# Seven block products in place of eight for the outputs of four tile pairs, with sums of blocks on VectorE

## The reference

```python
def _L0_cond_ref(x, c, weight, c_weight, bias):
    out = lax.conv_general_dilated(x, weight, window_strides=(STRIDE,), padding=[(PAD, PAD)], ..., feature_group_count=GROUPS)
    ctx = jnp.einsum('nd,od->no', c, c_weight)
    return out + ctx[:, :, None] + bias[None, :, None]

def _L0_ffn_ref(x, A_w, B_w, Wq_w, keys):
    q = jnp.einsum('bsd,rd->bsr', x, Wq_w)
    scores = jnp.einsum('bsr,er->bse', q, keys)
    top_vals, top_idx = jax.lax.top_k(scores, TOP_K)
    top_w = jax.nn.softmax(top_vals, axis=-1)
    gate = jnp.sum(jax.nn.one_hot(top_idx, NUM_EXPERTS) * top_w[..., None], axis=-2)
    z = jnp.einsum('bsd,nd->bsn', x, A_w)          # 64 experts of rank 8: 512 columns
    z_gated = (z.reshape(..., 64, 8) * gate[..., None]).reshape(..., 512)
    return jnp.einsum('bsn,on->bso', z_gated, B_w) * SCALING

x = x + _L0_ffn_ref(_L0_cond_ref(x, ...), A_w, B_w, Wq_w, keys)   # x: 32 x 64 x 1024
```

## Time and profile before

| | us |
|---|---|
| median of 3 runs (lowest, highest) | 234.68 (233.78, 234.82) |
| the profiled execution's own time | 234.61 |
| its span, first to last instruction | 232.8 |
| PE busy | 228.6 |
| PE weight loads busy | 204.4 |
| DVE busy | 172.9 |
| ACT busy | 113.2 |

### The profile page before, as it was taken

One profiled execution on the slowest core, in us unless ns is written; L12 is line 12 of the kernel. 1 busy time (PEld: TensorE's weight loads), 2 busy tenths in 40 slices (PEclk: granted clock), 3 DMA queues, 4 the chain that ended last, 5 costly groups with the idle time before them and its releaser, 6 DMA issues.

```text
span 232.8 us, 4002 instructions
## 1 busy us (share of the span) xinstructions
PE 228.6 (98%) x1381; PEld 204.4 (88%) x1381; DVE 172.9 (74%) x411; ACT 113.2 (49%) x293; POOL 7.7 (3%) x16
## 2 busy tenths in 40 slices
PE   8999999999999999999999999999999999999995
PEld 8999998888989989898898989889898989898884
DVE  2699889999878696977969587786958748827232
ACT  4996768265282562728356272735627262221000
POOL 2010071000000000000000000000000000000000
DMA  6999055742825538164553815545381433552632
GB/s 186 373 400 398 34 136 184 290 115 102 235 117 145 175 98 260 58 177 181 137 182 91 270 50 167 192 134 187 89 271 52 117 109 90 184 175 98 182 134 92
DMA packets 23780, 38.79 MB, mean 167 GB/s; under 512 B 2768, under 2 KB 11856, under 8 KB 23760
## 3 DMA queue, kind: packets, MB, share of 16 engines
q1 hardware_dynamic: 23616, 38.45, 50.8%
q10 hardware_dynamic: 144, 0.08, 0.2%
HBM read 25.94 MB, written 12.58 MB: 165 GB/s over the span
## 4 chain that ended last, share of the span: by engine, by line
PE 77%; DVE 15%; issue 3%; DMA 2%; ACT 2%; SPq 1%; DVEq 0%; ACTq 0%
PE p_z L686 30%; PE p_out L724 12%; PE p_out L725 12%; PE p_out L732 12%; PE p_conv L637 10%; DVE h_lo L801 3%; DVE h_t L841 2%; DMA x_blk<-in_x_blocks 2%; DVE a_lo L801 2%; DVE x_lo L801 2%; DVE z_g L926 1%; DVE a_raw L936 1%; ACT h_c L426 1%; ACT x_hi L390 1%; DVE b_lo L801 1%
## 5 line engine op out<-in xcount | busy, mean ns | idle before, releaser
L724 PE MATMUL p_out<-b_hi,zt_hi 128*128 128x512 f32 (+1 forms) x128 | 50.8, 398 | 0.3 <-DVE x_nat L944 0.3
L725 PE MATMUL p_out<-b_hi,zt_lo 128*128 128x512 f32 (+1 forms) x128 | 50.0, 392 | 0.0
L732 PE MATMUL p_out<-b_lo,zt_hi 128*128 128x512 f32 (+1 forms) x128 | 34.3, 391 | 0.0
L686 PE MATMUL p_z<-a_hi,h_hi 128*128 128x264 f32 x240 | 34.1, 285 | 0.1
L686 PE MATMUL p_z<-a_hi,h_lo 128*128 128x264 f32 x240 | 34.2, 285 | 0.0
L686 PE MATMUL p_z<-a_lo,h_hi 128*128 128x264 f32 x240 | 34.0, 284 | 0.0
L686 PEld LDWEIGHTS p_z<-a_hi,h_hi 128*128 128x128 f32 x240 | 31.9, 188 | 1.9 <-issue 0.8
L686 PEld LDWEIGHTS p_z<-a_hi,h_lo 128*128 128x128 f32 x240 | 31.2, 188 | 0.0
L686 PEld LDWEIGHTS p_z<-a_lo,h_hi 128*128 128x128 f32 x240 | 31.1, 188 | 0.0
L724 PEld LDWEIGHTS p_out<-b_hi,zt_hi 128*128 128x128 f32 x128 | 24.1, 188 | 6.0 <-issue 0.4
L732 PEld LDWEIGHTS p_out<-b_lo,zt_hi 128*128 128x128 f32 x128 | 23.8, 188 | 5.7
(11 more groups left out here) (109 smaller groups left out, 280.1 us busy)
## 6 DMA issues: line engine op xcount, KB each, us to landing
x_nat<-in_x_rows SPq DMA_DIRECT2D x16, 512.0 KB, 5.2
out_dram<-x_nat SPq DMA_DIRECT2D x31, 256.0 KB, 3.0
x_blk<-in_x_blocks SPq DMA_DIRECT2D x14, 516.0 KB, 3.6
z_dram<-a_raw SPq DMA_DIRECT2D x64, 64.0 KB, 1.8
...
```

Source lines behind the costliest of these rows:

```text
L686: mm = nc.tensor.matmul(z_bank(t, b)[:, 0:HB], h[:, t % 2, r, :], a[:, r, b * HB:(b + 1) * HB], start=k == 0 and r == 0, stop=k == 2 and r ...
L724: nc.tensor.matmul(dst, zt_hi[:, t % 2, c, :], b_hi[:, c, cols], start=c == 0, stop=False)
L725: nc.tensor.matmul(dst, zt_lo[:, t % 2, c, :], b_hi[:, c, cols], start=False, stop=False)
L732: mm = nc.tensor.matmul(dst, zt_hi[:, t % 2, c, :], b_lo[:, c, start:stop], start=False, stop=c == JC - 1)
```

## The change

Tiles 6 to 13 form four pairs (m = 0 to 3). A pair's gated z, 256 rows by 512, and B, 512 by 1024, are each cut into two by two blocks. In place of eight block products of 6 matmuls each there are seven (`product_1` to `product_7`), by sums of blocks:

- DVE sums blocks of B once (`sum_b`, in iterations 4 to 7), ACT and DVE split the four sums (`split_bt`). SP loads B again for it (`load_b`).
- For each pair DVE sums blocks of z (`sum_z31`, `sum_z2`, `sum_z4`); seven z blocks are split (`split_z1`, `split_z12`, `split_z34`, `split_z22`) where eight were.
- Partial sums that several outputs share are copied from one PSUM bank to another by ACT (`copy_xy`, `copy_yz`, `copy_zx`), and products are added on top of them. `add_5` adds one product to both tiles of the pair; `add_11`, `add_12`, `add_22` and `add_21` follow.
- In the loop, PE does products 1, 5, 2, 6 of pair m in iteration 9+2m and 7, 3, 4 in iteration 10+2m. Iterations 7 and 8 have one half of tile 5 each. `conv_sum` stands between the two banks of z from iteration 4 on.
- Room is made: `x_blk` has two slots from tile 5 on instead of three, `ones` and `cw` lie in `h_t`, `z_g` in `a_raw`, and later weights of the convolution in `h_c`.

The core of the diff:

```diff
+FP = 6
+NP = (NT - 2 - FP) // 2
+TB = 4
+LD = FP + 2 * NP
...
-        x_blk = sb("x_blk", [P, XB, XS + 2 * XO])
+        x_blk = sb("x_blk", [P, XB * XS])
...
+        zt_hi = sb("zt_hi", [P, 7, 2, P], F32R)
+        zt_lo = sb("zt_lo", [P, 7, 2, P], F32R)
+        bt_hi = sb("bt_hi", [P, 4, 2, J], F32R)
+        bt_lo = sb("bt_lo", [P, 4, 2, J], F32R)
...
+        b_sums = (a_raw[:, 3:5, 0:J], a_raw[:, 5:7, 0:J], h_c[:, 0].rearrange("p (a n) k -> p a (n k)", a=2))
+        z_sums = h_c[:, 0].rearrange("p (s tb) x -> p s tb x", s=2)
...
+        def pair_banks(m):
+            if m == NP - 1:
+                return p_conv[:, 0, :], p_conv[:, 1, :], p_conv[:, 2, :], p_t[:]
+            return p_out[:, 0, :], p_out[:, 1, :], p_conv[:, 2, :], p_t[:]
...
+                elif t >= FP + 2:
+                    m = (t - FP - 2) // 2
+                    sp.wait_ge(s_zsum, 3 * m + 3)
+                    sp.wait_ge(*((s_z22lo, m + 1) if t % 2 else (s_z1lo, m + 1)))
...
+            def split_z12(m):
+                if m:
+                    act.wait_ge(s_p6, m)
+                act.wait_ge(s_zsum, 3 * m + 2)
+                high(zt_at(zt_hi, 2, 2), sums_at(1), s_z12hi)
...
+            def split_bt(k):
+                act.wait_ge(s_btsum, k + 1)
+                high(bt_hi[:, k], b_sums[(0, 0, 1, 0)[k]], s_bthi)
+
+            def copy_xy(m):
+                x, y, _, _ = pair_banks(m)
+                act.wait_ge(s_p1, m + 1)
+                if m == 0:
+                    act.wait_ge(s_added, out_count(FP - 1, 1))
+                elif m < NP - 1:
+                    act.wait_ge(s_c12, m)
+                high(y, x, s_xy)
...
                 exp(i)
-                split_z(i - 1)
+                if i >= FP + 4 and i % 2 == 0:
+                    copy_zx(m)
+                if FP + 3 <= i < NT - 1 and i % 2:
+                    copy_xy(m)
+                if i == NT - 2:
+                    copy_xy(NP - 1)
+                if i <= FP:
+                    split_z(i - 1)
+                if i == FP + 1:
+                    split_z1(0)
+                if i >= FP + 2 and i % 2 == 0:
+                    split_z12((i - FP - 2) // 2)
+                if FP + 3 <= i < NT - 1 and i % 2:
+                    split_z34(m)
+                    split_z22(m)
                 if i + 3 < NT:
                     split_x(i + 3)
                 if i in (5, 7):
                     split_w(i // 2)
                     sum_w(i // 2)
-                if i == NT - 3:
-                    take_q(NT - 2)
                 if i + 2 < NT:
                     split_h(i + 2)
+                if TB <= i < TB + 4:
+                    split_bt(i - TB)
+                if FP + 3 <= i < NT - 1 and i % 2:
+                    split_z1(m + 1)
+                    copy_yz(m)
+                if i == NT - 2:
+                    split_z34(NP - 1)
+                    split_z22(NP - 1)
+            copy_yz(NP - 1)
+            split_z(NT - 2)
+            copy_zx(NP - 1)
             split_z(NT - 1)
...
-                            pe.wait_ge(s_zg, 2 * t)
+                            pe.wait_ge(s_zg, 2 * t - 1)
+                    if k == 0 and 1 not in banks and t >= 3:
+                        pe.wait_ge(s_zg, 2 * t)
...
+            def product_5(m):
+                pe.wait_ge(s_z12hi, m + 1)
+                pe.wait_ge(s_z12lo, m + 1)
+                if m:
+                    pe.wait_ge(s_vadd, m)
+                product(pair_banks(m)[2], 2, b_sum(0, m), False).then_inc(s_p5, 1)
...
+                m = (i - FP - 3) // 2
                 for k in range(3):
                     z_product(i, k, (1,), range(R))
+                if TS <= i < NT - 2:
+                    conv_sum(i + 2)
                 z_product(i, 0, (0,), range(R))
                 z_product(i, 1, (0,), range(R))
                 if i < TS:
                     turn_q(i)
                 z_product(i, 2, (0,), range(R))
-                if i + 2 < NT:
+                if i < TS:
                     conv_sum(i + 2)
                 scores(i)
-                if i >= NT - 2:
-                    out_part(i - 3, 1)
-                if i < NT - 1:
+                if i <= FP:
                     out_part(i - 2, 0)
-                if i + 2 < NT:
                     conv_pair(i + 2)
-                if i < NT - 3:
                     out_part(i - 2, 1)
-            out_part(NT - 3, 0)
-            out_part(NT - 3, 1)
-            out_part(NT - 2, 0)
+                elif i <= FP + 2:
+                    out_part(FP - 1, i - FP - 1)
+                    conv_pair(i + 2)
...
+                elif i % 2:
+                    product_1(m)
+                    product_5(m)
+                    conv_pair(i + 2)
+                    product_2(m)
+                    product_6(m)
+                else:
+                    product_7(m)
+                    product_3(m)
+                    conv_pair(i + 2)
+                    product_4(m)
             out_part(NT - 2, 1)
             out_part(NT - 1, 0)
             out_part(NT - 1, 1)
...
+            def sum_z31(m):
+                a = FP + 2 * m
+                dve.wait_ge(s_zi, 16 * (a + 2))
+                step = JQ + 64
+                ends = a_raw[:].rearrange("j r x -> j (r x)")[:, 0:2 * step].rearrange("j (s x) -> j s x", s=2)
+                ends = ends[:, :, 0:J].rearrange("j s (tb x) -> j s tb x", tb=4)[:, :, :, 0:64]
+                nc.vector.tensor_tensor(z_sums[:, :, :, 0:64], ends, zt_half(a + 1, 0).unsqueeze(1).to_broadcast([P, 2, 4, 64]),
+                                        ALU.subtract).then_inc(s_zsum, 1)
+
+            def sum_z2(m):
+                dve.wait_ge(s_zsum, 3 * m + 1)
+                nc.vector.scalar_tensor_tensor(out=z_sums[:, 1, :, 64:P], in0=zt_half(FP + 2 * m, 0), scalar=-1.0,
+                                               in1=z_sums[:, 1, :, 0:64], op0=ALU.mult, op1=ALU.subtract).then_inc(s_zsum, 1)
+
+            def sum_b(k):
+                dst, other = ((0, 1), (0, 2), (1, 2), (0, 1))[k]
+                for load in ((0, 1), (2,), (), (3,))[k]:
+                    dve.wait_ge(s_bt[load], 16)
+                nc.vector.tensor_tensor(b_sums[dst], b_sums[dst], b_sums[other], ALU.add).then_inc(s_btsum, 1)
...
+            def add_5(m):
+                a, cols = FP + 2 * m, slice(J, 2 * J)
+                dve.wait_ge(s_p5, m + 1)
+                dve.wait_ge(*rows_come(a))
+                dve.wait_ge(*rows_come(a + 1))
+                both = x_nat[:, a % XN:a % XN + 2, cols]
+                nc.vector.scalar_tensor_tensor(out=both, in0=pair_banks(m)[2].unsqueeze(1).to_broadcast([P, 2, J]), scalar=-SCALING,
+                                               in1=both, op0=ALU.mult, op1=ALU.add).then_inc(s_vadd, 1)
...
             split_z(1)
+            add(0, 0)
             split_h(4)
-            add(0, 0)
             for i in range(3, NT):
+                m = (i - FP - 3) // 2
                 if i + 3 < NT:
                     differ(i + 3, 0)
                 copy_scores(i)
...
                 if i + 3 < NT:
                     differ(i + 3, 1)
                 take_first(i)
-                if i < NT - 3:
+                if i <= FP + 1:
                     add(i - 3, 1)
+                if FP + 5 <= i < NT - 1 and i % 2:
+                    add_21(m - 1)
                 top_second(i)
                 take_second(i)
                 weigh(i)
                 invert(i)
                 gate(i)
                 turn_z(i)
-                if i >= NT - 3:
-                    add(i - 3, 1)
                 if i + 2 < NT:
                     turn_h(i + 2, 0)
                     turn_h(i + 2, 1)
-                split_z(i - 1)
+                if i <= FP:
+                    split_z(i - 1)
                 if i == 3:
                     split_keys()
                 if i in (5, 7):
                     split_w(i // 2)
                     split_ws(i // 2)
-                add(i - 2, 0)
+                if i <= FP + 1:
+                    add(i - 2, 0)
+                if i == FP + 1:
+                    split_z1(0)
+                if TB <= i < TB + 4:
+                    sum_b(i - TB)
+                if i == FP + 2:
+                    sum_z31(0)
+                    add(FP - 1, 1)
+                    sum_z2(0)
+                    sum_z4(0)
+                elif i >= FP + 4 and i % 2 == 0:
+                    sum_z31(m + 1)
+                    add_12(m)
+                    sum_z2(m + 1)
+                    add_22(m)
+                    sum_z4(m + 1)
+                elif FP + 3 <= i < NT - 1:
+                    add_5(m)
+                    split_z34(m)
+                    split_z22(m)
+                    add_11(m)
+                if i >= FP + 2 and i % 2 == 0:
+                    split_z12((i - FP - 2) // 2)
                 if i + 3 < NT:
                     split_x(i + 3)
                 if i in (4, 6):
                     sum_w(i // 2)
```

(16 more changed lines are left out.)

342 lines of the change are left out of this document (283 added, 59 removed).

## The result

| | before | after |
|---|---|---|
| median, us | 234.59 | 244.44 |
| lowest, highest | 233.78, 234.82 | 242.07, 245.94 |
| profiled execution, span | 234.61, 232.8 | 243.17, 241.3 |
| PE, DVE, ACT busy | 228.6, 172.9, 113.2 | 227.5, 195.5, 126.9 |

The runs of before are those of the prediction and one more beside after. The change makes the kernel slower: ratio 1.0349, 95% interval 1.029 to 1.0407. That ratio is made of the two runs of after with the highest clock (242.07 and 243.17 us). The four runs are ordered by TensorE's mean granted clock: 0.993 gave 242.07 us, 0.986 gave 243.17, and 0.972 gave 245.72 and 245.94. The first two lie inside the stated range of 235.9 to 243.5 us, the other two above it.

The account below looks back on a forecast made before the run. PE bounds the kernel before; after, DVE's cycle to x_lo exceeds PE's shorter iterations. 234.61 - 5.58 (matmuls) - 0.3 (`add(0, 0)`) + 11.75 (waits) = 240.5 us, range 235.9 to 243.5.

Parts of the forecast that it names:

- Direction and mechanism: Slower: DVE's longer list delays x_lo, so PE waits at the third `conv_sum` matmul; chance 0.82 of over 0.5% slower.
- 24 matmuls off PE, 5.58 us: On PE, 42 output matmuls a pair for 48; four pairs at 0.2325 us a matmul save 5.58 us.
- DVE's cycles: From one third `conv_sum` matmul to the next through DVE: 13.46 to 14.46 us in iterations 5 to 12; waits total 11.75.
- a small sum: On DVE, a 256-element sum of z blocks: priced 0.34 us, possibly up to 0.45, as a gating half.
- side remark on records taken as spacing: On DVE, taking the longer record lengths as spacing between starts would add an estimated 1 to 1.5 us.
- x_hi behind zt_hi: On ACT in iterations 8, 10, 12, x_hi stands behind zt_hi; DVE itself would reach x_lo 0.6 us earlier.
- the milder rival: On ACT, x_hi is not held up behind zt_hi: waits 9.5 us, time 238.2; chance 0.20 for 236 to 238.5.
- -0.3 us for `add(0, 0)`: Putting `add(0, 0)` ahead of `split_h(4)` removes the 0.34 us for which PE waited; counted as -0.3 us.
- a sign against it: The prediction is wrong if, among other signs, stretches before 95 us differ from before by over a microsecond.
- The stalls cost more than they last: Rival: PE's waits of 3.2 and 3.6 us lower TensorE's clock, 2.9 us per fall, 246 us; chance 0.04.
- the gain arrives: Rival: DVE's reserve (26 us against 21.6) suffices, x_lo is in time at `conv_sum`, 228.7 us; chance 0.12.
- Edits at nothing: PSUM copies on ACT, the query chain (ends A+2.6, scores at A+3.15) and the tail after the last scores cost nothing.

Follow-up runs that it names:

- experiment 1: Changed kernel plus matmuls nobody reads, ahead of `conv_sum` in iterations 8, 9 (ten each), 11 and 13 (six each); 240.41 us.
- experiment 12: Against 9: bt_hi behind the next iteration's exp on ACT, bt_lo ahead of the next sum_b on DVE, fourth B load moved; 228.72 us.
- experiment 4: Kernel before the change, with only `conv_sum` moved between the banks of z from iteration 4 on; 234.09 us, ratio 0.9984.
- experiment 2: Changed kernel with x_hi ahead of zt_hi on ACT in iterations 8, 10 and 12, nothing else moved; 239.43 us.
- experiment 11: As 9, but with B's sums in iterations 4 to 7, where the change has them; 234.79 us.
- 7: Changed kernel, DVE's list reordered: x_lo first, query steps earlier in even iterations, ACT's `split_z12` behind `split_h`; B's sums in iterations 4 to 7; 234.74 us.
- Experiments 3: Changed kernel with `conv_sum` back behind both banks of z; 238.07 us.
- experiments 5: Changed kernel with x_lo right behind `turn_h` on DVE, and x_hi ahead of the z sums' split on ACT; 239.19 us.
- 8: As 7, but with B's sums one iteration earlier, in iterations 3 to 6; 233.18 us.
- 9: As 8, with `split_q` before `split_h` in every iteration and an add between `turn_q` and `split_q`; 233.35 us.

## Why the prediction was right, and where it fell short

*Direction and mechanism: right.* The forecast was slower, by DVE's longer list ahead of x_lo, with PE standing at the third matmul of `conv_sum`. The time of 240.5 us is 3.9 us under the median of 244.44, which lies 0.9 us above the range; the two runs with the higher clock, 242.07 and 243.17, lie in it. That experiment 1, without a fall of the clock, comes to within 0.1 us of the sum is in part luck: its waits are 0.6 us longer than forecast and its start is some 0.3 us shorter.

- **24 matmuls off PE, 5.58 us.** Experiment 12 bears it out. From the scores of iteration 4 to those of iteration 15 its trace takes 139.41 us, for 144.58 before: 5.17 less. Iterations 8 and 9 pay back 0.7, and moving `conv_sum` gives some 0.4 by itself (experiment 4): 5.58 + 0.4 - 0.7 is 5.3. (The medians, 234.71 and 228.72, are 5.99 us apart; the profiled execution, at 229.51, was the slowest of five.) The spacing of 0.2325 us was the right price.
- **DVE's cycles.** The predicted 14.03, 14.03, 14.46, 14.46, 13.83 and 14.46 us were 14.09, 14.10, 14.56, 14.60, 13.87 and 14.63 with the clock kept up. Six cycles of some twenty pieces each are within 0.17 us. Start-to-start prices from rows add up. The waits that follow from them and the prediction's iterations of PE are 12.33 us for 11.75. One price was low: sum_z2 takes 0.45 us and not 0.34 (126.85 to 127.30 above), the upper value that the prediction gave for a small sum. Its side remark on records taken as spacing was low too: by its own lists they would add some 2 to 3 us and not 1 to 1.5. Nothing rests on it.
- **x_hi behind zt_hi.** Said to cost 0.6 us of DVE's time, and by the prediction's list 1.16 in iteration 8, where there is one add fewer. Experiment 2 took 0.7 to 0.8 off each of the three cycles, 2.2 us together, for 2.3 forecast by the milder rival. In iteration 8 less came off than was listed, since DVE's zt_lo still waits for ACT's zt_hi there and the small sums are dearer. That x_hi would itself release PE, at the first matmul of `conv_sum`, was not foreseen; it does not change the sum.
- **-0.3 us for `add(0, 0)`.** Too small: the scores of iteration 4 come at 64.43 us in after and at 65.55 before. That is 1.1 us, just over the microsecond that the prediction named as a sign against it. The other kernels with the same start have 64.0 to 65.0, so this part also varies by itself. The change has other matmuls on `ones` at the start as well, and no experiment tells the two apart.
- **The clock: the missing term.** The sum counted a wait at its length. "The stalls cost more than they last" was a rival with 0.04. It should have been a term, for the sum itself forecast waits of 3.2 and 3.6 us in two iterations running, a pattern that no row of before contains. Not having seen a fall was taken as evidence against one, where it was only that PE hardly idles in the loop of the kernel before. Its price of 2.9 us a fall was too high for after, where one costs 1.52 us (experiment 1 against after), as the lower level lasts 3.4 us and not for a whole bank of z. It can come near: in experiment 2's iteration 8 it lasts 6.8 us, over all of bank 0, and costs 2.6 (16.70 us for 14.10). And it depends on the place. In experiment 11 the clock falls just behind the scores of iteration 8, and the next iteration takes 12.67 us; in 7, without a fall, 12.66. There DVE's cycle is longer than PE's work even at the lower level. Two falls in after are 3.0 us of the profiled execution: 240.5 + 3.0 + 0.6 for the waits - 0.8 for the start is 243.3, and it took 243.17. Runs at a mean clock of 0.972 spent twice as long at the lower level as the profiled one at 0.986, which fits their 2.6 us more, but they have no trace here; it is argued, not shown.
- **The rival "the gain arrives", 228.7 us.** It did not happen in the change, and it was there to be had: experiment 12 runs at 228.72 us. Its reasoning by totals (26 us of reserve against 21.6 of work) was sound about what is possible and wrong about what the written order does.
- **"Edits at nothing".** The query chain was put at zero because it ended before the scores. That held, but by little: 0.55 us in the prediction, 0.9 in after (in iteration 8 q_t is done at 118.93 and the scores start at 119.86). Experiments 3 and 5, which made x_lo early, ran straight into it. A cover of under a microsecond should be named as the next bound.

My expectations of experiments 5, 7, 8 and 9 were all too low by about 3 us for one reason: they looked at the wait that was to vanish and not at the place where the displaced work would stand. Experiment 12 was the one for which both lists were laid out to the end of the iteration, and the one where the expectation was passed.
